# Layer 0 attention of a four-layer cross-attention kernel: scores one unit further ahead, and one copy split over two engines

## The reference

```python
h = jnp.concatenate([x, latents], axis=1)
q = (latents @ q_w + q_b).reshape(b, k_len, NH, DH)
kv = (h @ kv_w + kv_b).reshape(b, p + k_len, NH, DH, 2)
kmat, v = (kv[..., 0], kv[..., 1])
attn = jnp.einsum('bkhd,bnhd->bhkn', q, kmat) / DH
full_mask = jnp.concatenate([attention_mask.astype(bool), jnp.ones((b, k_len), bool)], axis=-1)
attn = jnp.where(full_mask[:, None, None, :], attn, -jnp.inf)
attn = jax.nn.softmax(attn.astype(jnp.float32), axis=-1).astype(q.dtype)
attn_out = jnp.einsum('bhkn,bnhd->bkhd', attn, v).reshape(b, k_len, H)
attn_out = attn_out @ out_w + out_b + residual
out = rmsnorm(attn_out, postnorm_w)
out = jax.nn.gelu(out @ mlp_w1 + mlp_b1) @ mlp_w2 + mlp_b2
```

## Time and profile before

| what | value |
|---|---|
| median of three runs | 840.12 us (840.08 to 841.82) |
| profiled execution, time | 840.74 us |
| profiled execution, span | 839.0 us |
| mean granted clock of PE over the span | 0.937 of full |
| busy: PE, DVE, ACT, POOL | 87%, 64%, 48%, 43% of the span |
| layer 0 attention units, first score to last turn | 14.2 to 200.0 us |

### The profile page before, as it was taken

The page is one execution under the profiler, slowest core; times in us unless marked ns, Lnnn a source line. Parts: engine busy times, 40 slices in busy tenths (PEclk is TensorE's granted clock), DMA queues, the critical chain, the costliest instruction groups (busy, mean ns, idle before and its releaser), DMA issues.

```text
span 839.0 us, 12837 instructions
## 1 busy us (share of the span) xinstructions
PE 730.8 (87%) x4752; PEld 556.6 (66%) x4752; DVE 532.9 (64%) x1034; ACT 403.9 (48%) x965; POOL 360.2 (43%) x383
## 2 busy tenths in 40 slices
PE   8888888876399888779999999999998799776798
PEld 6676666654289445557875787876677688344598
DVE  6577776753844599955537674433888557398644
ACT  3687878854231377645652233653242131376421
POOL 2487554543700488844315561000765502177200
PEclk9899999967699999989999999999999899996899
DMA  8200000000000600002432000332000000200000
GB/s 318 95 1 1 2 1 2 2 1 2 0 1 1 201 1 2 1 1 92 161 103 98 1 1 1 101 104 97 1 0 1 1 1 1 100 1 1 1 20 32
DMA packets 24957, 32.51 MB, mean 39 GB/s; under 512 B 2752, under 2 KB 19392, under 8 KB 24768
## 3 DMA queue, kind: packets, MB, share of 16 engines
q1 hardware_dynamic: 24336, 31.10, 10.9%
q10 hardware_dynamic: 560, 0.59, 0.2%
HBM read 30.64 MB, written 1.05 MB: 38 GB/s over the span
## 4 chain that ended last, share of the span: by engine, by line
PE 62%; DVE 18%; POOL 8%; issue 7%; ACT 4%; DMA 1%; SPq 0%; POOLq 0%; DVEq 0%
PE wide_ps L432 9%; PE narrow_ps L451 8%; PE wide_ps L741 7%; PE wide_ps L692 6%; PE wide_ps L479 5%; PE narrow_ps L776 5%; POOL probs L1514 4%; PE wide_ps L715 4%; PE wide_ps L728 4%; DVE scoresb L1207 2%; DVE mx L1216 2%; PE narrow_ps L599 2%; DVE sums L1223 2%; PE wide_ps L412 2%; POOL probs L1500 2%
## 5 line engine op out<-in xcount | busy, mean ns | idle before, releaser
L479 PE MATMUL wide_ps<-ident,probs 128*128 128x128 f32 x640 | 96.3, 291 | 49.0 <-POOL probs L1500 23.1
L1492 POOL TENSOR_TENSOR scoresb<-scoresb,mx 128x768 f32<-128x768 f32 (+1 forms) x40 | 70.7, 1767 | 153.0 <-DVE mx L1214 115.4
L479 PEld LDWEIGHTS wide_ps<-ident,probs 128*128 128x128 f32 x640 | 77.2, 150 | 79.2 <-issue 63.2
L1514 POOL TENSOR_TENSOR probs<-scoresb,rcp 128x512 f32<-128x512 f32 (+1 forms) x128 | 89.4, 720 | 71.3 <-DVE rcp L1291 70.1
L897 ACT ACTIVATE probsT<-wide_ps 128x1024 f32<-128x1024 f32 (+1 forms) x73 | 64.3, 881 | 114.9 <-PE wide_ps L479 114.7
L1478 POOL TENSOR_TENSOR rstd<-veps,mhalf 128x1 f32<-128x1 f32 x56 | 32.0, 572 | 136.1 <-DVE veps L1142 136.1
L1500 POOL TENSOR_TENSOR probs<-scoresb,rcp 128x1024 f32<-128x1024 f32 x40 | 78.2, 1954 | 7.6 <-DVE rcp L1224 7.6
L432 PE MATMUL wide_ps<-xq_r,wstream_r 128*128 128x512 f32 x192 | 65.3, 424 | 8.7 <-issue 6.9
L451 PEld LDWEIGHTS narrow_ps<-wstream_r,hidden 128*128 128x128 f32 x576 | 69.2, 188 | 1.2 <-DVE xB L1170 0.5
L451 PE MATMUL narrow_ps<-wstream_r,hidden 128*128 128x256 f32 x576 | 69.7, 281 | 0.3 <-DVE xB L1170 0.3
L970 ACT ACTIVATE scoresb<-wide_ps,mx 128x320 f32<-128x320 f32 x128 | 66.4, 531 | 1.9 <-DVE mx L1287 1.6
(11 more groups left out here) (163 smaller groups left out, 1625.5 us busy)
## 6 DMA issues: line engine op xcount, KB each, us to landing
wstream<-in_L_xattn_wk SPq DMA_DIRECT2D x8, 512.0 KB, 4.0
wstream<-in_L_xattn_wv SPq DMA_DIRECT2D x8, 512.0 KB, 5.2
wstream<-in_L_xattn_wo SPq DMA_DIRECT2D x8, 512.0 KB, 6.4
wstream<-in_wqT SPq DMA_DIRECT2D x8, 512.0 KB, 7.5
wstream<-in_L_xattn_mlp_w SPq DMA_DIRECT2D x2, 1024.0 KB, 10.7
wstream<-in_L_xattn_w_fc SPq DMA_DIRECT2D x2, 1024.0 KB, 6.2
rows<-in_rows SPq DMA_DIRECT2D x1, 1280.0 KB, 14.0
xq<-in_x SPq DMA_DIRECT2D x1, 1024.0 KB, 11.8
```

The costliest lines, as they stand in the source:

```text
L479: m = nc.tensor.transpose(ps[:, j * P:(j + 1) * P], probs[:, u % 2, j * P:(j + 1) * P], ident[:])
L1492: g.tensor_tensor(s3[:, first:], s3[:, first:], mx[:, u % 3, first:].unsqueeze(2).broadcast_to([P, 16 - first, n_scores]), ALU.subtract).t ...
L1514: g.tensor_tensor(probs[:, u % 2, o:o + 2 * n].rearrange("p (i k) -> p i k", i=2), s3[:, :, lo:hi], rcp[:, u % 3, 0:2].unsqueeze(2).broadc ...
```

## The change

Four edits, all in layer 0.

1. Four score buffers in place of three (`RING0`), laid over the same memory; the small tiles of maxima, sums and reciprocals follow (`pair_of`). Everything that had an index modulo 3 has one modulo 4.
2. `AHEAD0 = 3`: on PE the score in step s is that of unit s+4 (was s+3), on ACT the exponentials are those of unit s+3 (was s+2), on DVE the front is that of unit s+3 (was s+2) and the reciprocal that of unit s+2 (was s+1). The loops start one step earlier. The two PSUM slots for scores stay two.
3. The copy of the turned probabilities is divided: ACT copies four blocks (512 columns), DVE the fifth (128 columns, `probs_turned0`).
4. On DVE that copy stands first in the step, ahead of the front.

```diff
+        RING0, AHEAD0 = 4, 3
+        def scores_of(u):
+            return scoresb[:].rearrange("p a n -> p (a n)")[:, u % RING0 * 2 * KEYS0:(u % RING0 + 1) * 2 * KEYS0]
+        def pair_of(tile, u, o=0):
+            o += u % RING0 * 8
+            return tile[:].rearrange("p a n -> p (a n)")[:, o:o + 2]
+        DIVIDE0 = 4
...
-                ps, filled = take_wide(("T", u), among=TURNS)
+                ps, filled = take_wide(("T", u), 2 if u < len(units0) else 1, among=TURNS)
...
-            for step in range(-3, n0 + 3):
+            for step in range(-1 - AHEAD0, n0 + 3):
...
-                if step + 3 < n0:
-                    scores0(step + 3)
+                if step + 1 + AHEAD0 < n0:
+                    scores0(step + 1 + AHEAD0)
...
-                n = 5 if u < len(units0) else 8
+                n = DIVIDE0 if u < len(units0) else 8
...
-                if u >= 3:
-                    act.wait_ge(prob_ready, probcount[u - 2])
+                if u >= RING0:
+                    act.wait_ge(prob_ready, probcount[u - RING0 + 1])
...
-                if step + 2 < n0:
-                    exp0(step + 2)
+                if step + AHEAD0 < n0:
+                    exp0(step + AHEAD0)
...
-                if u >= 3:
-                    dve.wait_ge(*wide.empty(("S", u - 3)))
+                if u >= RING0:
+                    dve.wait_ge(*wide.empty(("S", u - RING0)))
...
+            def probs_turned0(u):
+                key = ("T", u)
+                dve.wait_ge(*wide.full(key))
+                v.tensor_copy(turned_probs(u)[:, DIVIDE0 * P:5 * P], wide_ps[:, wide.slot(key), DIVIDE0 * P:5 * P]
+                              ).then_inc(wide.drained[wide.slot(key)], 1)
...
-            for step in range(-2, n0 + 5):
+            for step in range(-AHEAD0, n0 + 5):
...
-                if step + 2 < n0:
-                    front0(step + 2)
-                if 0 <= step + 1 < n0:
-                    middle0(step + 1)
+                if 0 <= step < n0:
+                    probs_turned0(step)
+                if step + AHEAD0 < n0:
+                    front0(step + AHEAD0)
+                if 0 <= step + AHEAD0 - 1 < n0:
+                    middle0(step + AHEAD0 - 1)
```

More of the change, by code:

```diff
@@ L966, in exp0 @@
                 act.wait_ge(max_ready, u + 1)
-                if u >= 3:
-                    act.wait_ge(prob_ready, probcount[u - 2])
+                if u >= RING0:
+                    act.wait_ge(prob_ready, probcount[u - RING0 + 1])
                 for i in range(2):
-                    nc.scalar.activation(scoresb[:, u % 3, i * KEYS0:(i + 1) * KEYS0],
+                    nc.scalar.activation(scores_of(u)[:, i * KEYS0:(i + 1) * KEYS0],
                                          wide_ps[:, wide.slot(key), i * 512:i * 512 + KEYS0], ACT.Exp,
-                                         scale=1.0 / 16, bias=mx[:, u % 3, i:i + 1],
-                                         accum_out=sums[:, u % 3, i:i + 1]).then_inc(wide.drained[wide.slot(key)], 1)
+                                         scale=1.0 / 16, bias=pair_of(mx, u)[:, i:i + 1],
+                                         accum_out=pair_of(sums, u)[:, i:i + 1]).then_inc(wide.drained[wide.slot(key)], 1)
             def exp(u, n):
@@ L1004, in _ @@
             n0 = len(units0)
-            for step in range(-2, n0 + 2):
+            for step in range(-AHEAD0, n0 + 2):
                 if step == 0:
@@ L1283, in front0 @@
                                      mask0[:, b, :].unsqueeze(1).broadcast_to([P, 2, T]), ALU.add))
-                if u >= 3:
-                    dve.wait_ge(*wide.empty(("S", u - 3)))
-                link(v.tensor_reduce(mx[:, u % 3, 4:6], ps[:, :, 0:KEYS0], AX, ALU.max))
-                v.tensor_scalar(mx[:, u % 3, 0:2], mx[:, u % 3, 4:6], -1.0 / 16, None, ALU.mult).then_inc(max_ready, 1)
+                if u >= RING0:
+                    dve.wait_ge(*wide.empty(("S", u - RING0)))
+                link(v.tensor_reduce(pair_of(mx, u, 4), ps[:, :, 0:KEYS0], AX, ALU.max))
+                v.tensor_scalar(pair_of(mx, u), pair_of(mx, u, 4), -1.0 / 16, None, ALU.mult).then_inc(max_ready, 1)
+            def probs_turned0(u):
[3 more added lines that the diff above has]
+                              ).then_inc(wide.drained[wide.slot(key)], 1)
             def middle0(u):
                 dve.wait_ge(*wide.empty(("S", u)))
-                v.reciprocal(rcp[:, u % 3, 0:2], sums[:, u % 3, 0:2]).then_inc(rcp_ready, 1)
+                v.reciprocal(pair_of(rcp, u), pair_of(sums, u)).then_inc(rcp_ready, 1)
             dve.wait_ge(load["cols"], 16)
@@ L1510, in normalize0 @@
                     pool.wait_ge(*wide.full(("T", u - 2)))
-                s3 = scoresb[:, u % 3, 0:2 * KEYS0].rearrange("p (i k) -> p i k", i=2)
+                s3 = scores_of(u).rearrange("p (i k) -> p i k", i=2)
                 for lo, hi, o in ((0, S, 0), (S, KEYS0, 2 * S)):
@@ L1514, in normalize0 @@
                     g.tensor_tensor(probs[:, u % 2, o:o + 2 * n].rearrange("p (i k) -> p i k", i=2), s3[:, :, lo:hi],
[L1515 removed]
+                                    pair_of(rcp, u).unsqueeze(2).broadcast_to([P, 2, n]), ALU.mult).then_inc(prob_ready, 1)
             def spread_keys(layer, kbd, mask, heads_):
```

## The result

| kernel | median, us | ratio to before, 95% interval |
|---|---|---|
| before | 840.45 | 1 |
| changed | 903.41 (896.64 to 904.74) | 1.073 (1.0675 to 1.0785) |

The change makes the kernel 7.3% slower. The forecast was 888 with a range of 864 to 908.

What follows compares the result with a forecast made beforehand. No engine is full; a loop of waits sets the pace. Block 0 11.7, blocks 1 and 2 26.8, block 3 6.3 sum to 44.8; with 3.5 for the clock, +48 on 840.7: 889, or 888 against the median, range 864 to 908.

Steps and rivals of the forecast that it cites:

- rival 3: Layer 0: PE at half clock for half of it, 0.75 as mean; +48 + 25, about 912; chance 0.08.
- Its own signs: Turns end near 245, full blocks near 58, DVE's copy waits nearly every step, POOL idles 4 to 5 at projections.
- Side gate: On PE, a side product awaiting DVE's side copy starts 2.30 after the same step's turn (q 2.5, k 2.2).
- score gate: Score of s+4 on PE waits for exponentials, front and turn of s-1: 2.82 after that turn, before 1.88.
- A block step by step: Turn-to-turn times of a full block's 16 steps, together 56.7 against 43.3 worked out for before: 13.4 longer.
- the clock: Layer 0: PE at half clock for 10% more of the time, about 1 a block; 3.5 added over the layer.
- Block 0 with the start: First block of layer 0, no projections, second part of the first products starting 3.1 later: 11.7 longer in all.
- blocks 1 and 2: The two full blocks of layer 0, each 13.4 longer: 26.8.
- block 3: Last block of layer 0: projections +4.5, 12 units at 2.33 against 2.18 before, +1.8; together +6.3.
- The projection term: At a block's two projections, statistics and next normalise stand behind the turn: 5.9 and 6.3, before 4.6 and 3.6; +4.5.
- Rival 1: Layer 0: only the wait before scores counts, side copies' wait mostly hidden; about 22 more, so 862; chance 0.14.
- Rival 2: Layer 0: reciprocal one unit further ahead, PE's 21.8 of waiting for probabilities goes; 819 to 825; chance 0.04.

## Why the prediction was right

**The number, and luck.** 903.4 lies in the range of 864 to 908, but near its end: it is 15 above the forecast of 888 and 9 below the 912 of rival 3. What the prediction gives for the upper end, a copy of 0.42 (+10), reaches 899 and did not come: the copy took less than was put on it. So the mechanism is right, and that the time is still inside the range is in part luck. Its own signs came out the same way: the turns end at 266 where near 245 was said, the full blocks take 67 and 65 where it was near 58, while DVE waits in 55 of 64 units (1.9 each), POOL idles over 4 at a projection, and the rest of the program is as long as before within 2.

**The place and the mechanism.** DVE's copy of the fifth block waits for the turn, and four things stand behind it. The waits, the timelines and the experiments say so: with that call last the kernel is faster than before, with all else as changed.

**The pieces.** The new copy was taken at 0.22 a step with 0.1 and 0.42 as ends; the next instruction starts 0.20 after it (207.28 to 207.48), its duration is 0.29, that of the mask on as many columns. The estimate of 0.26 from the Trainium skill (Perfetto Trace Analysis, Optimizing Scalar/DVE Operations) lies between the two. Side gate 2.30, measured 2.30, behind `q` 2.5 and 2.49, behind `k` 2.2 and 2.16; score gate 2.82, measured 2.76 to the end of the exponentials.

**A block step by step.** The intervals of turn ends in the third block, worked out and measured:

| from unit | 32 | 33 | 34 | 35 | 36 | 37 | 38 | 39 | 40 | 41 | 42 | 43 | 44 | 45 | 46 | 47 |
|---|---|---|---|---|---|---|---|---|---|---|---|---|---|---|---|---|
| worked | 3.0 | 2.0 | 5.9 | 6.3 | 4.5 | 4.3 | 3.5 | 3.7 | 3.05 | 1.55 | 3.4 | 2.7 | 3.7 | 3.65 | 1.55 | 3.9 |
| measured | 3.1 | 2.1 | 6.0 | 7.1 | 4.6 | 5.9 | 3.5 | 4.8 | 3.8 | 1.7 | 3.5 | 4.1 | 3.6 | 4.6 | 1.7 | 4.9 |
| clock | 0.79 | 1.00 | 1.00 | 0.53 | 0.99 | 0.71 | 0.96 | 0.50 | 0.78 | 1.00 | 0.93 | 0.65 | 1.00 | 0.71 | 0.79 | 0.75 |

Nine of 16 agree within 0.2. The last row is the granted clock of each interval: the nine have 0.79 to 1.00, the seven that don't agree 0.50 to 0.78. Five of the seven (from 35, 37, 39, 45 and 47) also end in a turn that takes 1.24 or more instead of 0.7, that is one at half clock. So the working holds where PE is at full clock, and what it is short by stands where PE is not. The sum is 65.3 against 56.7.

**The step that was mis-sized: the clock.** The prediction put 3.5 on it, "1 a block", from PE's share of a step and 10% more time at half clock. The traces have 31 us at half clock in layer 0 before and 106 after (turn of unit 0 to that of unit 63), that is 18% and 45% of it, so 27 more in a hundred and not 10, and turns that took over 1 us went from 7 to 22 of 64. Six filling transposes at ten places of a full block gave 14.6 back (12 by the ratios), where 3.5 was the whole term. The error had two parts. I took the lower clock from the last stretch's 0.82 at 68% busy as if busy share alone gave it, and the blocks came to 0.73 to 0.80 with PE, as I put it, at 66% of full-clock work. And I counted only turns and sides as longer; scores and values are too, and a longer turn moves every gate behind it. No run parts these two. Rival 3, half of layer 0 at half clock and 0.75 as mean, describes the clock better than the forecast does (45%, blocks of 0.73 to 0.80); its price of 25 more was too high: 16 were missing. It had a chance of 0.08.

**The sum by pieces.** Block 0 with the start was forecast +11.7 and is +21.2, blocks 1 and 2 +26.8 and +41.6, block 3 +6.3 and +3.2, the rest 0 and -2.0; the clock had 3.5 as a term of its own. The time at half clock grew where the forecast is short: from 7 to 24 in block 0, from 10 to 64 in blocks 1 and 2, from 14 to 18 in block 3.

**The start.** Forecast 3.1 at the first turn, measured 5.0 (31.4 against 26.4): the value product begins 3.6 later, since the score of unit 2 itself stands ahead of it too, and takes 1.6 longer at half clock.

**Block 3** was forecast +6.3 and is +3.2. The projection term is there: the two intervals of the projection take 12.8 instead of 8.5, so 4.3. (The prediction added 4.5, while its own four figures, 5.9 and 6.3 against 4.6 and 3.6, give 4.0.) The wrong part is the working of before: it had 2.18 a unit without sides before and 2.33 after. Over the last 11 intervals the trace has 2.36 after, as worked out, but 2.50 before, so these units got faster and not slower. The working was at full clock, while the trace of before stands at 0.82 in that stretch; no run shows whether that is the reason.

**The rivals.** Rival 1 (side gate hidden) is refuted by the kernel with the side copy first. (Its 862 takes 5 for a full block where its text says 7; with 7 it would be 869, still far from 903.) Rival 2 (faster, 15 to 21) is there as a gain of 10 in the kernel that is only further ahead, under the condition that the prediction gave it: fronts that are not held. In the changed kernel they are held. The rule behind it is that consistent bubbles can mean too few buffers (the Trainium skill, Perfetto Trace Analysis, Optimization Strategy). Here the fourth buffer and the further distance together go with 1.2% once nothing on DVE waits for the turn ahead of the front, and only part of that lies in layer 0; with the wait at the head the kernel that has them is 7.3% slower than before.

**Too bold.** That a fourth buffer gains nothing because the score slots in PSUM stay two was too bold taken by itself: the kernel that has it and no wait at the head is 1.2% faster, though less than half of that lies in layer 0 in the profiled execution.

## What to carry to other kernels

On an engine that works in order, ask of each new wait what stands behind it and who waits for that, before asking what the instruction costs: 0.2 us of copy a step cost 63 us at the head of a step, some 10 in its middle against its end, and nothing to be seen at its end. Splitting a copy over two engines makes the second engine wait for the producer, so put its part behind all work that others wait for. And where a change adds gaps on TensorE, price its products at the lower clock as well: here at least a fifth of the loss was that.

## What the runs showed of the hardware that was not expected

TensorE made 60 more instructions in each full block and the kernel got 14.6 us faster, the granted clock going from 0.73 and 0.79 in the changed kernel to 0.92. The traces show the clock at two levels, half and full, and nothing between; the means are shares of time. Two falls in the changed kernel stand beside gaps shown above. At 18.27 the clock fell to half behind PE's gap of 2.50, and a product took 3.51 instead of 1.90. At 212.83 it fell within the gap of 2.00, with one of 0.85 shortly before it: the granted clock is 1.00 from 206.0 to there and 0.50 to 216.2, and the side product and the turn in it take 1.28 and 1.27, where 0.76 and 0.71 are the lengths at full clock.
